# Making both steps of each square layer together, product by product, in a fused attention and gated MLP kernel

## The reference

```python
xn = layernorm(x)
# attention without softmax: phi = elu + 1, 16 heads of 16
q, k, v = split(xn @ W_qkv.T + b_qkv); q, k = phi(q), phi(k)
a = (q @ (k.T @ v)) / clip(q . sum(k), 1e-6)
a = layernorm(a @ W_proj.T + b_proj) * gamma + beta + xn
# gated MLP, ternary weights (-1, 0, 1), a scale for each output column
h = silu(xn @ w1.T * s1) * (xn @ w2.T * s2)          # 256 -> 1024
h = gelu(h @ h1.T * t1)                              # 1024 -> 1024, square
h = gelu(h @ h2.T * t2)                              # 1024 -> 1024, square
out = x + a + h @ w3.T * s3                          # 1024 -> 256
```

## Time and profile before

| | us |
|---|---|
| median of 3 runs (lowest, highest) | 1477.41 (1475.27, 1477.58) |
| the profiled execution | 1476.11 |
| its span, first to last instruction | 1474.3 |
| busy: PE, DVE, ACT, POOL | 1465.8, 1161.3, 935.6, 466.8 |

### The profile page before, as it was taken

The page is one execution under the profiler, slowest core; times in us unless marked ns, Lnnn a source line. Parts: engine busy times, 40 slices in busy tenths (PEclk is TensorE's granted clock), DMA queues, the critical chain, the costliest instruction groups (busy, mean ns, idle before and its releaser), DMA issues.

```text
span 1474.3 us, 33305 instructions
## 1 busy us (share of the span) xinstructions
PE 1465.8 (99%) x11020; PEld 1269.2 (86%) x11020; DVE 1161.3 (79%) x2090; ACT 935.6 (63%) x1727; POOL 466.8 (32%) x554
## 2 busy tenths in 40 slices
PE   9999999999999999999999999999999999999998
PEld 5997988979798797988979889798897988979887
DVE  6857778787887877878788787887878878787787
ACT  4556657666575766757657666575765667666564
POOL 2213415234151341504325043240523415234141
PEclk9999999999999999999999999999999999999999
DMA  8796845727366373663727548185481854827444
GB/s 239 233 311 238 281 145 182 259 93 269 127 215 231 105 266 114 237 212 113 259 110 264 185 141 286 58 278 174 147 297 47 279 170 165 277 68 253 160 160 158
DMA packets 85058, 287.66 MB, mean 195 GB/s; under 512 B 7456, under 2 KB 45984, under 8 KB 61728
## 3 DMA queue, kind: packets, MB, share of 16 engines
q0 software_dynamic: 43296, 231.75, 46.0%
q1 hardware_dynamic: 40896, 54.29, 11.2%
q10 hardware_dynamic: 832, 1.18, 0.2%
HBM read 270.42 MB, written 25.17 MB: 200 GB/s over the span
## 4 chain that ended last, share of the span: by engine, by line
PE 99%; DVE 1%; ACT 0%; issue 0%; DVEq 0%; ACTq 0%
PE ps L1042 53%; PE ps L1015 8%; PE ps L1013 7%; PE ps L1127 7%; PE ps L902 4%; PE ps L904 4%; PE ps L903 4%; PE ps L1075 4%; PE ps L965 2%; PE ps L954 2%; PE ps L975 1%; PE ps L924 1%; PE ps L1098 1%; PE ps L896 0%; PE ps L1152 0%; DVE values_a L1736 0%
## 5 line engine op out<-in xcount | busy, mean ns | idle before, releaser
L1042 PE MATMUL ps<-operands_a,hidden_weights 128*128 128x256 f32 x2520 | 367.9, 285 | 0.0
L1042 PE MATMUL ps<-lo_a_in_bits,hidden_weights 128*128 128x256 f16 x2520 | 337.1, 273 | 0.0
L1042 PEld LDWEIGHTS ps<-operands_a,hidden_weights 128*128 128x128 f32 x2520 | 323.5, 189 | 1.4 <-DVE partial_sums L1783 0.2
L1783 DVE TENSOR_TENSOR partial_sums<-partial_sums,ps 128x512 f32<-128x512 f32 x300 | 204.2, 685 | 119.4 <-PE ps L1042 69.2
L1745 DVE SCALAR_TENSOR_TENSOR lo_a_in_bits<-values_a,operands_a 128x512 f16<-128x512 f32 x315 | 236.6, 773 | 42.0 <-POOL values_a L775 20.5
L1042 PEld LDWEIGHTS ps<-lo_a_in_bits,hidden_weights 128*128 128x128 bf16 x2520 | 232.6, 98 | 35.1 <-DVE lo_a_in_bits L1745 3.2
L783 POOL DMA_DIRECT2D hidden_weights<-weight_blocks x236 | 135.6, 575 | 383.4 <-PE ps L1042 359.4
L1383 ACT ACTIVATE operands_a<-values_a 128x512 fp32r<-128x512 f32 x180 | 112.9, 627 | 70.3 <-POOL values_a L760 18.9
L760 POOL TENSOR_TENSOR values_a<-values_a 128x512 f32<-128x512 f32 x30 | 38.4, 1281 | 357.1 <-DVE values_a L1736 338.1
L1015 PE MATMUL ps<-xnT,w_ffn 128*128 128x512 f32 x512 | 150.5, 421 | 0.0
L1042 PE MATMUL ps<-operands_b,hidden_weights 128*128 128x256 f32 x840 | 146.8, 296 | 0.0
(11 more groups left out here) (162 smaller groups left out, 2735.6 us busy)
## 6 DMA issues: line engine op xcount, KB each, us to landing
hidden_weights<-weight_blocks POOLq DMA_DIRECT2D x180, 1024.0 KB, 5.3
hidden_weights<-weight_blocks POOLq DMA_DIRECT2D x60, 512.0 KB, 3.9
raw_weights<-weight_blocks SPq DMA_DIRECT2D x42, 347.5 KB, 3.0
hidden_weights<-in_w_ffn POOLq DMA_DIRECT2D x16, 512.0 KB, 8.0
weight_blocks<-weight_sums SPq DMA_DIRECT2D x16, 512.0 KB, 3.3
weight_blocks<-in_w_ffn SPq DMA_DIRECT2D x16, 512.0 KB, 10.3
out_dram<-acc SPq DMA_DIRECT2D x31, 256.0 KB, 2.2
x<-in_H SPq DMA_DIRECT2D x15, 512.0 KB, 5.4
```

Source lines behind the costliest of these rows:

```text
L1042: r = mm(bank[:, m * HT:(m + 1) * HT], wk, xk, start=i in firsts and begins and m == 0 and j == 0, stop=i in lasts and ends and m == 1 and ...
L1783: v.tensor_tensor(scratch[:, dst, :], scratch[:, kept, :], product_bank(s, i), ALU.add).then_inc(add.sem, 1)
```

## The change

Both sets of a layer now run together, product by product: (0, 1), (1, 1), (0, 5), (1, 5), ... in the order 1, 5, 6, 7, 2, 3, 4 (PAIRED). products() makes one product for both sets of a pair: the first kind (hi or lo) for the even set, then for the odd one, then the second kind for both. The weights lie in DRAM in this order, and the ring's turns are of seven entries of it, which no longer are the products of one set. The even set's sums stay in partial_sums; the odd set's first two rows are in the two buffers of gate_ring, the third in a new buffer. All differences of H0 and H1 are made by POOL. The bank of each product, the order of every queue and what each sum waits for are rewritten for this; the weight check is cut in six pieces rather than four. ScalarE's order, not shown, follows the products in the same way; in layer one it has hi_of_lower of G1, keep_first of sets 0 and 1, hi of G1's T3, residual, hi of G1's T4, rows_hi twice, and then gelu and hi in the order of the blocks C22, C11, C12, C21. The last tile's own orders are gone.

```diff
-RING_ORDER = (1, 5, 6, 7, 2, 4, 3)
+ORDER = (1, 5, 6, 7, 2, 3, 4)
+PAIRED = tuple((s, i) for p in range(2) for i in ORDER for s in (2 * p, 2 * p + 1))
 RING_PARTS = ((0, 1), (1, 2), (3, 2), (5, 2))
-PART_OF = {1: 0, 5: 1, 6: 1, 7: 2, 2: 2, 4: 3, 3: 3}
+
...
-ORDER = ((1, 5, 6, 7, 2, 4, 3), (1, 6, 2, 5, 7, 3, 4), (1, 5, 6, 2, 7, 4, 3), (1, 6, 2, 5, 7, 3, 4))
-BANKS = ((4, 5, 0), (1, 2, 3), (4, 5, 0), (1, 2, 3))
-PART_FREE = ((1, 6, 2, 3), (1, 5, 7, 4), (1, 6, 7, 3), (1, 5, 7, 4))
...
+BANKS = ((4, 2, 0), (5, 3, 1)) * 2
...
-CHECKS = 4
+CHECKS = 6
...
+    second_sums = sb("second_partial_sum", [P, N])
...
+    def partial(s, n):
+
+        if s % 2 == 0:
+            return scratch[:, n, :]
+        return second_sums[:] if n == 2 else gate[:, n, :]
...
+    def ring_part_free(t, turn, g):
+
+        s, i = PAIRED[turn * PRODUCTS + sum(RING_PARTS[g]) - 1]
+        return prod.after(t, f"{s}P{i}")
...
-            def refill(t, s, g):
-
-                pool.wait_ge(*prod.after(t, f"{s}P{PART_FREE[s][g]}"))
-                if g == 0:
-                    pool.wait_ge(s_copied[(s + 1) % SETS], 64)
+            def refill(t, turn, g):
+
+                pool.wait_ge(*ring_part_free(t, turn, g))
+                if g == 0 and turn % 2 == 1:
+                    pair = (turn + 1) % SETS // 2
+                    pool.wait_ge(s_copied[2 * pair], 64)
+                    pool.wait_ge(s_copied[2 * pair + 1], 64)
                 pool.sem_inc(refill_begun.sem, 1)
-                pool.dma_start(of_ring(ring, g), part_weights((s + 1) % SETS, g)).then_inc(ring_loaded[g].sem, 16)
+                pool.dma_start(of_ring(ring, g), part_weights((turn + 1) % SETS, g)).then_inc(ring_loaded[g].sem, 16)
...
+                pool.wait_ge(s_copied[1], 64)
...
                     if filling:
                         refill(t, 0, 1)
                         refill(t, 0, 2)
-                    t1(t, "H0")
-                    t2(t, "H0")
-                    if filling:
-                        refill(t, 0, 3)
                     if more:
                         ln1(t + 1)
                     if filling:
+                        refill(t, 0, 3)
                         refill(t, 1, 0)
-                    t3(t, "H0")
+                    inverse_root(t, 1, ln2_var, ln2_root)
                     if filling:
                         refill(t, 1, 1)
-                    t4(t, "H0")
+                        refill(t, 1, 2)
+                    t1(t, "H0")
+                    t1(t, "H1")
                     if filling:
-                        refill(t, 1, 2)
                         refill(t, 1, 3)
-                    inverse_root(t, 1, ln2_var, ln2_root)
+                    t2(t, "H0")
+                    t2(t, "H1")
+                    if filling:
+                        refill(t, 2, 0)
+                    t3(t, "H0")
                     t3(t, "H1")
                     if filling:
-                        refill(t, 2, 0)
+                        refill(t, 2, 1)
+                    t4(t, "H0")
                     t4(t, "H1")
                     if filling:
-                        refill(t, 2, 1)
                         refill(t, 2, 2)
                         refill(t, 2, 3)
...
-                def product(t, s, i, parts=HI_FIRST):
-
-                    quarter_product(t, s, i, 0, parts[0], begins=True)
-                    quarter_product(t, s, i, 1, parts[0])
-                    quarter_product(t, s, i, 0, parts[1])
-                    quarter_product(t, s, i, 1, parts[1], ends=True).then_inc(prod.sem, 1)
+                def products(t, pair, i, parts):
+
+                    for part in parts:
+                        for s in (2 * pair, 2 * pair + 1):
+                            quarter_product(t, s, i, 0, part, begins=part == parts[0])
+                            r = quarter_product(t, s, i, 1, part, ends=part == parts[1])
+                            if part == parts[1]:
+                                r.then_inc(prod.sem, 1)
 
...
-                    quarter_product(t, 0, 1, 0, 0, begins=True)
-                    quarter_product(t, 0, 5, 0, 0, begins=True)
-                    quarter_product(t, 0, 6, 0, 0, begins=True)
-                    quarter_product(t, 0, 1, 0, 1)
-                    quarter_product(t, 0, 5, 0, 1)
-                    quarter_product(t, 0, 6, 0, 1)
-                    quarter_product(t, 0, 1, 1, 1)
-                    quarter_product(t, 0, 1, 1, 0, ends=True).then_inc(prod.sem, 1)
-                    quarter_product(t, 0, 5, 1, 0)
-                    quarter_product(t, 0, 6, 1, 0)
-                    quarter_product(t, 0, 5, 1, 1, ends=True).then_inc(prod.sem, 1)
-                    quarter_product(t, 0, 6, 1, 1, ends=True).then_inc(prod.sem, 1)
+                    products(t, 0, 1, HI_FIRST)
+                    products(t, 0, 5, LO_FIRST)
                     to_rows(t, 0)
                     to_rows(t, 1)
-                    product(t, 0, 7)
-                    product(t, 0, 2)
-                    product(t, 0, 4)
-                    product(t, 0, 3)
-
-                    product(t, 1, 1, LO_FIRST)
-                    product(t, 1, 6)
+                    products(t, 0, 6, HI_FIRST)
                     proj_step(t, 0)
                     proj_step(t, 1)
-                    product(t, 1, 2)
-                    product(t, 1, 5, LO_FIRST)
-                    product(t, 1, 7)
-                    product(t, 1, 3, LO_FIRST)
-                    product(t, 1, 4)
-
-                    product(t, 2, 1, LO_FIRST)
-                    product(t, 2, 5)
-                    product(t, 2, 6)
+                    products(t, 0, 7, HI_FIRST)
+                    products(t, 0, 2, LO_FIRST)
+                    products(t, 0, 3, HI_FIRST)
+                    products(t, 0, 4, LO_FIRST)
+
+                    products(t, 1, 1, HI_FIRST)
+                    products(t, 1, 5, LO_FIRST)
+                    products(t, 1, 6, HI_FIRST)
                     if more:
-                        product(t, 2, 2)
-                        product(t, 2, 7)
                         transposes(t + 1, 0)
                         transposes(t + 1, 1)
-                    else:
-                        quarter_product(t, 2, 2, 0, 0, begins=True)
-                        quarter_product(t, 2, 2, 0, 1)
-                        product(t, 2, 7)
-                        quarter_product(t, 2, 2, 1, 0)
-                        quarter_product(t, 2, 2, 1, 1, ends=True).then_inc(prod.sem, 1)
-                    product(t, 2, 4)
-                    product(t, 2, 3)
-
-                    product(t, 3, 1, LO_FIRST)
-                    product(t, 3, 6)
-                    product(t, 3, 2, LO_FIRST)
-                    product(t, 3, 5)
-                    product(t, 3, 7, LO_FIRST)
-                    product(t, 3, 3)
-                    product(t, 3, 4, LO_FIRST)
+                    products(t, 1, 7, HI_FIRST)
+                    products(t, 1, 2, LO_FIRST)
+                    products(t, 1, 3, HI_FIRST)
+                    products(t, 1, 4, LO_FIRST)
                     if more:
...
                     swap(t, 1)
-                    add_u(t, 0)
                     lo(t, "G1", "T3", first > 0)
                     lo(t, "G0", "B21", first > 0)
                     lo(t, "G1", "B21", first > 0)
+                    rows_lo(t, 0)
+                    rows_lo(t, 1)
+                    add_u(t, 0)
+                    add_u(t, 1)
+                    lo(t, "G0", "B22", first > 0)
+                    lo(t, "G1", "B22", first > 0)
+                    if more:
+                        ln1_stats(t + 1)
                     add_w(t, 0)
+                    add_w(t, 1)
+                    add_c22(t, 0)
+                    add_c22(t, 1)
                     lo(t, "G0", "T4", first > 0)
                     lo(t, "G1", "T4", first > 0)
-                    add_c22(t, 0)
-                    lo(t, "G0", "B22", first > 0)
-                    lo(t, "G1", "B22", first > 0)
-                    rows_lo(t, 0)
-                    add_c12(t, 0)
-                    add_c21(t, 0)
+                    ln2_stats(t)
                     if checking and more:
                         check_piece(t - 1, 0)
-                    rows_lo(t, 1)
-                    if more:
-                        ln1_stats(t + 1)
-
-                    add_u(t, 1)
-                    ln2_stats(t)
-                    add_v(t, 1)
+                    add_c12(t, 0)
+                    add_c12(t, 1)
                     lo(t, "H0", "B11", first > 0)
+                    lo(t, "H1", "B11", first > 0)
+                    add_c21(t, 0)
+                    add_c21(t, 1)
+
...
```

299 lines of the change are left out of this document (129 added, 170 removed).

## The result

The changed kernel takes 1580.64 us (median of 4, 1578.80 to 1585.44) against 1477.03 (1475.27 to 1477.58): ratio 1.0709, 95% interval 1.0683 to 1.0734. The prediction was 1499 us, 1481 to 1520: the sign was right, the loss is 104 us in place of 22, far above the range.

What follows compares the result with a forecast made beforehand. TensorE, busy 99% of the span, was taken as the bound. Per tile 1.5 + 0.1 + 0.25 - 0.48 = 1.4 us, 21 over 15 tiles, plus 0.6 at the end, gave 22 us more: 1499 us, range 1481 to 1520.

Steps and rivals of the forecast that it cites:

- The weight ring: Second layer, set 3's first product: PE waits 1.5 us per tile for refill(1, 1), queued behind inverse_root; ends 0.1 and 2.4.
- Six small checks for four: nothing: VectorE's weight checks, six small ones replacing four: no cost, with DVE's time filled to 79%.
- T1 and T2 of H1 to POOL: nothing, the cover is 7.3 us, and the chain ends 1.2 us early: Border of first and second layers: moving these differences from VectorE to GpSimd costs nothing; PE waits if cover is too short.
- DVE or ScalarE at the border of the layers: Sign against the forecast: PE waiting for these engines there would mean the chains through gelu were misjudged.
- The clock: PE's granted clock in the square layers: read as 1.00, the 2.4 GHz level, with no loss in the sum.
- proj_step: After the pair's third product: PE waits 0.25 us per tile for the second rows_lo; ends 0 and 0.6.
- The first fill of the ring: Once in a run: fill ends near 123, PE first wants it at 135.34; costs nothing, cover 12 us.
- The gain in the layers: Within layers, operands used twice in a row are wanted half as fast: 0.48 us of PE lateness per tile goes; ends 0 and 0.48.
- The sum: Whole kernel: 1.4 us more per tile, 21 over 15 tiles, plus 0.6 at the end: 22 us more.
- The rivals: Wait doesn't come, 1472 (0.15); short wait, 1485 to 1490 (0.09); ring doesn't recover, 1521 and over (0.11); does nothing, 1477 (0.05).
- the ring doesn't recover: Rival: the next three ring parts land 0.5 us late each, 1.5 us more per tile: 1521 and over; chance 0.11.

Runs made afterwards that it cites:

- the last run: Paired kernel with late check, turns and refitted queue orders (1490.00 us), second layer's layer-norm root moved further back on GpSimd, behind refill(2, 1): 1472.95 us.
- the turns alone: Changed kernel plus three GpSimd waits in the second layer, so T2, T3, T4 of H0 wait for VectorE's lo's of H1's T1, T2, T3: 1569.22 us.
- the run with all orders: Changed kernel with late check, GpSimd waits, root behind refill(1, 1), and ScalarE and VectorE queues reordered, residual behind rows_hi: 1552.39 us.

## Why the prediction was wrong

- **The weight ring: right, in mechanism, place and size.** 1.5 us of wait in each of 15 tiles were forecast; 26.0 / 15 = 1.73 were measured, one hi run into the second layer, behind the root (GpSimd, changed kernel), inside its own bounds of 0.1 and 2.4:

```profile
655.62 1.43 POOL L746 TENSOR_TENSOR rstd<-var_plus_eps,power 128x4 f32<-128x4 f32 x1 [5.31 <-DVE minus_mean L1597]
657.71 1.25 POOL L783 DMA_DIRECT2D hidden_weights<-weight_blocks  x2 [0.38 <-issue]
```

- **"Six small checks for four: nothing" failed, and it is the largest term.** The step looked at VectorE's busy share. But the loads of the pieces are a series, each behind the check before it, now six long in place of four, and a check that comes before its load has landed stops the queue. Moving two checks gave 48 us of the 104: about 30 of waits for relu_tmp and hidden_out, 11 of waits for VectorE's sums and 7 of clock, less 3 more for the weights.
- **"T1 and T2 of H1 to POOL: nothing, the cover is 7.3 us, and the chain ends 1.2 us early" failed.** The prediction gives the end of this chain and not its terms, and it names no wait of VectorE on GpSimd. In the changed kernel it gave way at add_u(2) (22 us); with the weights in time PE waited 46.5 us for lo's of the second layer; in the old order the same move costs 33 us, most of it by ScalarE's queue. A row of the prediction had the sign of it: the lo of G1's T1 took 1.11 us where others take 0.68, and it was used as a number, not asked why.
- **Product 7's bank** (add_u(2) has to read product 6 first) and the chain through add_c12, gelu, hi and q_act to kv_step were not in the sum at all. The text named "DVE or ScalarE at the border of the layers" as what would prove it wrong; no price stood for it in the range.
- **The clock** was taken as 1.00 throughout. It fell to 0.50 after ten of the waits of 1.75 to 2.1 us, and 17.4 us (the estimate above) went with it.
- **proj_step:** 0.25 us a tile forecast, 6.4 / 15 = 0.43 measured, within its ends. **The first fill of the ring** was put at nothing, and was nothing: its last part landed at 127.54, later than the forecast's 123, and PE's first product of tile 1 starts at 136.45, without a wait.
- **The gain in the layers was right in sign.** Every tile but the first takes 90.3 to 90.8 us in the last run, where the kernel before has 90.6 to 91.0; 0.3 to 0.4 us a tile of the 0.48 claimed. How much of this is the pairing and how much the new orders of the queues, no run separates.
- **The sum was wrong as a sum.** It added waits of one path as if they were independent. Taking away the predicted one alone brought 1587 for 1581 us; taking away the weights, the sums and the checks together brought 1583. Only with the other causes gone did the root's way back pay: its last move brought 17 us, from 1490 to 1473, and that by the differences behind it, not by the weights.
- **The rivals** all turned on the same weight part; none had VectorE's queue in it. 1521 and over, "the ring doesn't recover", came nearest in time and is not what happened: the next parts were in time (24.1 us in 14 waits, one a tile).

What stays open: the prices of the single causes are not separable, as each moves the others; what decides whether the clock falls after a wait; and why the turns alone came out 11 us above their expectation, beyond the longer wait for hidden_out.

## What to carry to other kernels

When work is regrouped, lay out every queue that gets a denser stretch, not only the engine that sets the end, and price each wait on a buffer that is loaded again only after its last reader: its period is the load, the read and the read's wait in its queue, whatever the busy share. On a path where three engines pass work on, a wait that is removed shows the next; look for it before pricing the gain, and judge a new order only when its queues have been fitted to it. An experiment that moves one instruction moves everything behind it in its queue: read from the trace which of these the wait ended on, and not from the time alone.

## What the runs showed of the hardware

- VectorE instructions with two operands in SBUF waited for GpSimd's running difference, and were passed over when GpSimd's next instruction followed within some 0.02 us, even with a DMA issue between two differences: 4.05 us for 0.68. Sums with one operand in PSUM didn't wait (0.688 us beside a difference, 0.682 otherwise).
- After some waits of 1.75 to 2.1 us, 0.1 to 1.1 us after their end, the granted clock fell to 0.50 for a while. The ten stretches of this kind cost about 17 us, an estimate, so about 1.7 us each, as much as the wait. Not every wait did it: ten of the changed kernel's 41 waits of over 1 us did, none of those for partial_sums among them, and the run with all orders (1552 us), with 15 waits of up to 1.7 us for relu_tmp, kept 0.999. What decides was not followed up. With no wait left, in the last run, it was 1.00.
- A load of 232 KB by SyncE's queue, 3.0 us as the median of 70, took 5.15 us beside two parts of the ring.
